# Single-pass up products, a shorter join and smaller rings in a fused graph-attention and feed-forward kernel

## The reference

```python
x = x + gnn(layernorm(x), src, dst, W, attn_l, attn_r, W_res)     # x: 50000 x 768, 25000 edges sorted by dst
x = x + ffn(layernorm(x)[None], ...)[0]
# gnn: ft = x_head @ W.T for 12 heads of 64; e = leaky_relu(a1[src] + a2[dst]);
#      alpha = softmax of e over the edges with one dst; agg = segment_sum(alpha * ft[src], dst)
#      return relu(agg + x_head @ W_res.T)
# ffn: gelu(x @ W1 + b1) @ W2 + b2 for all rows but the first six, which go through small experts
```

## Time and profile before

| what | value |
|---|---|
| median of 3 runs | 2991.76 us (2991.27 to 2992.91) |
| the profiled execution | 2989.99 us, span 2988.1 us |
| TensorE, share of the span | 96%, granted clock 0.978 |
| VectorE, ScalarE, GpSimd | 83%, 62%, 71% |
| VectorE uses the first scale (L1009) | at 46.56 us |
| edge loop, 600 to 1100 us | TensorE busy 499.88, VectorE 455.79, DMA share 0.78 |
| drain and join, 1130 to 1240 us | TensorE busy half of the time, clock 1.00 falling to 0.50 |
| node loop, 1500 to 2000 us | TensorE busy 498.94, VectorE 422.88, DMA share 0.87 |
| node loop, 1300 to 1350 us | TensorE busy 50.00 of 50, DMA share 0.94 |

### The profile page before, as it was taken

How to read it: one execution, slowest core, us unless ns; L and a number is a source line. 1 busy time by engine, 2 the same in 40 slices (tenths; PEclk the granted TensorE clock), 3 DMA queues, 4 the chain that set the end, 5 groups by cost and what they waited for, 6 DMA issues and landing times. The chain is left out here.

```text
span 2988.1 us, 65135 instructions
## 1 busy us (share of the span) xinstructions
PE 2866.0 (96%) x20124; PEld 2556.8 (86%) x20124; DVE 2486.9 (83%) x5828; ACT 1843.7 (62%) x3384; POOL 2125.9 (71%) x2027
## 2 busy tenths in 40 slices
PE   3999999999999996699999999999999999999998
PEld 3888888888888884588888888999989999899986
DVE  5699999999999976688888888888888888888883
ACT  2566666656666561467666767666676666667662
POOL 6766666666666610688888888888888888888882
PEclk9999999999999997699999999999999999999998
DMA  8899999898888725599888888888888888888873
GB/s 203 153 220 224 211 218 219 210 219 218 217 220 212 219 92 194 185 324 320 315 308 311 301 310 295 309 296 302 297 294 304 294 299 294 290 293 291 301 247 117
DMA packets 246616, 757.82 MB, mean 254 GB/s; under 512 B 78899, under 2 KB 81203, under 8 KB 246291
## 3 DMA queue, kind: packets, MB, share of 16 engines
q1 hardware_dynamic: 173900, 544.41, 51.5%
q0 software_dynamic: 69312, 209.33, 30.7%
q10 hardware_dynamic: 3176, 1.29, 0.2%
HBM read 623.04 MB, written 232.17 MB: 286 GB/s over the span
## 5 line engine op out<-in xcount | busy, mean ns | idle before, releaser
L670 ACT ACTIVATE arena<-ps 128x768 f32<-128x768 f32 x392 | 317.8, 811 | 532.5 <-PE ps L730 532.3
L891 PE MATMUL ps<-wr_bd,arena 128*128 128x128 f32 x4704 | 601.7, 278 | 27.5 <-DVE arena L1214 26.4
L891 PEld LDWEIGHTS ps<-wr_bd,arena 128*128 128x128 f32 x4704 | 566.8, 194 | 36.6 <-issue 34.6
L870 PE MATMUL ps<-arena,w_sb 128*96 128x256 f32 x2352 | 571.6, 379 | 0.0
L582 POOL DMA_INDIRECT arena<-agg_scratch,nrow x392 | 441.0, 1125 | 79.8 <-issue 73.2
L1209 DVE SCALAR_TENSOR_TENSOR ps<-ps,r_n,arena 128x768 f32<-128x768 f32 x392 | 400.8, 1022 | 62.5 <-DMA arena<-agg_scratch,nrow 39.3
L870 PEld LDWEIGHTS ps<-arena,w_sb 128*96 128x96 f32 x2352 | 362.3, 163 | 82.8
L560 POOL TENSOR_SCALAR arena<-csr_neg,mv,r_n 128x768 f32<-128x768 f32 x392 | 387.2, 988 | 50.9 <-POOL r_n L590 41.4
L621 ACT ACTIVATE arena<-ps 128x512 f32<-128x512 f32 x588 | 312.8, 593 | 119.9 <-PE ps L747 70.2
L1214 DVE SCALAR_TENSOR_TENSOR arena<-ps,arena 128x768 f32<-128x768 f32 x392 | 375.4, 958 | 13.4
L572 POOL TENSOR_SCALAR arena<-arena,nm_n,r_n 128x768 f32<-128x768 f32 x392 | 383.1, 977 | 1.0 <-issue 0.4
(11 more groups left out here) (198 smaller groups left out, 5526.6 us busy)
## 6 DMA issues: line engine op xcount, KB each, us to landing
arena<-in_x SPq DMA_DIRECT2D x196, 768.0 KB
arena<-in_x_cols SPq DMA_DIRECT2D x392, 384.0 KB
out<-arena SPq DMA_DIRECT2D x195, 768.0 KB, 5.2
agg_scratch<-arena SPq DMA_DIRECT2D x196, 384.0 KB
arena<-in_x,e_slot POOLq DMA_INDIRECT x392
arena<-agg_scratch,nrow POOLq DMA_INDIRECT x392
nrow<-row_scratch SPq DMA_DIRECT2D x196, 1.0 KB
row_scratch<-e_slot POOLq DMA_INDIRECT x189
```

The costliest lines, as they stand in the source:

```text
L870: last = nc.tensor.matmul(ps[0:HID, 6 + v, 0:PAIR * P], w1_sb[:, i, :], t2[:, v, i, :], start=(i == 0), stop=(i == NC - 1))
L891: last = nc.tensor.matmul(pair(1)[:, i * P:(i + 1) * P], xt_ring[:, g, i * P:(i + 1) * P], wr_bd[:], start=True, stop=True)
```

## The change

1. **Up as single-pass products.** w1 and the transposed tile are split into a high and a low part in `fp32r`: `w1_hi`, `w1_lo`, `t2_hi`, `t2_lo`. ScalarE writes `t2_hi` from PSUM, VectorE the rest into `t2_lo`, and up is hi*hi + lo*hi + hi*lo. `pair(0)` comes free only after `t2_lo`.
2. **Statistics.** bn_stats and its aggregate leave the node loop's VectorE; ScalarE does the copy with sum and the square for all tiles.
3. **Two masks.** dst transpose and mask move from step 9 to step 20, and `mask_ring` has 2 slots.
4. **Aggregated rows.** `agg_ring` has 2 rows; the last 10 chunks use 5 rows in the free end of `xs_ring`. SP waits for these before it loads x over them.
5. **Join in row layout.** Coefficients are transposed to chunks x heads, the last and first rows are scaled as they lie (98 x 1536), only the keep coefficient is spread over the features, one scan per feature block runs straight from PSUM, and the rows are transposed back and combined in two halves.
6. **First power.** For group 0 both powers are issued at GpSimd's step 8 and not 11 and 12.

The distances of gather, residual product and power in the node loop stay as they are. Core of the diff:

```diff
-        mask_ring = part(32424, BODY, P)
-        agg_ring = part(37544, G, D)
+        mask_ring = part(32424, 2, P)
+        agg_ring = part(35752, AR, D)          # AR = 2
+        agg_last = part(6912, LR, D)           # LR = 5, NL = 10
...
+                    if isinstance(b, int) and c == G + 1:
+                        pool.wait_ge(s_ve, 1)
+                        pool.tensor_tensor(r_a[:, 0, 0:2 * G:2], ve_a[:, 0, 0:2 * G:2], half[:, 0:G], ALU.pow)
+                        pool.tensor_tensor(r_a[:, 0, 1:2 * G:2], ve_a[:, 0, 1:2 * G:2], half[:, 0:G], ALU.pow)
...
# ScalarE, node loop
-                        nc.scalar.activation(t2[:, v, :, k * P:(k + 1) * P], pair(0)..., ACT.Copy)
+                        nc.scalar.activation(t2_hi[:, v, :, k * P:(k + 1) * P], pair(0)..., ACT.Copy)
-                    if u % PAIR == 1 and exists(t, NT):
+                    if exists(t, NT):                        # L701, and likewise L663
...
# TensorE, node loop
-                        at_least(pe, s_te2, tt)
+                        at_least(pe, s_lo2, tt)
                         transposes(pair(0), n2[:, (u - L_T2) % 2, :], s_tp2)
-                            last = nc.tensor.matmul(ps[0:HID, 6 + v, 0:PAIR * P], w1_sb[:, i, :], t2[:, v, i, :], ...)
+                            for n, (w, h) in enumerate(((w1_hi, t2_hi[:, v]), (w1_lo, t2_hi[:, v]), (w1_hi, t2_lo[:, v]))):
+                                last = nc.tensor.matmul(ps[0:HID, 6 + v, 0:PAIR * P], w[:, i, :], h[:, i, :], ...)
...
# VectorE, node loop, between y and the small tiles
+                        dve.wait_ge(s_te2, tl + 1)
+                        V.tensor_tensor(t2_lo[:, v, :, f], pair(0)..., t2_hi[:, v, :, f].bitcast(f32),
+                                        ALU.subtract).then_inc(s_lo2, 1)
-                        V.tensor_scalar(ve_n[:, w, 0:1], mv1[:, w, 1:2], EPS, None, ALU.add)
-                            V.bn_stats(bn1[:, u // PAIR % 2, h, :], x_ring[...])
-                        V.bn_aggr(mv1[:, w, 0:2], ...)
...
# VectorE, edge loop
-                        at_least(dve, d_agg[j], 16 * (2 * b + (i - L_AGG) // G))
+                        if not isinstance(b, int) or ca < EC - NL:
+                            at_least(dve, d_agg[v % AR], 16 * (BODY // AR * b + (i - L_AGG) // AR))
+                        elif ca >= EC - NL + LR:
+                            dve.wait_ge(d_agl[(ca - EC + NL) % LR], 16)
...
# join, VectorE
-            for j in range(NC):        # product, scan, product, product, add on 128 x 196
+            dve.wait_ge(d_last, 16)
+            V.tensor_tensor(o_last, o_last, coef_t[:, :, 0, :]..., ALU.mult)          # 98 x 1536
+            for j in range(NC):
+                V.tensor_tensor_scan(chain_o[:, j, 1:EC + 1], keep_b[:, j, :], ps[:, j // 2, ...], 0.0, ALU.mult, ALU.add)
+            for n in range(2):
+                V.tensor_tensor(fix_rows[:, n, :], back, coef_t[:, n, 1, :]..., ALU.mult)
+                V.tensor_tensor(fix_rows[:, n, :], fix_rows[:, n, :], o_first[:, n, :], ALU.add).then_inc(s_frow, 1)
```

More of the change, by code:

```diff
@@ L162, in gnn_ffn_kernel @@
         g_f = part(18856, EC, rows=HEADS)
[L163 to L167, removed]
+        coef_t = part(19052, 2, 3, HEADS, rows=EH)
+        chain_o = part(27000, NC, EC + 1)
+        keep_b = part(28200, NC, EC)
         o_last = part(22292, 2, D, rows=EH)
@@ L170, in gnn_ffn_kernel @@
         fix_rows = part(25364, 2, D, rows=EH)
[L171 to L175, removed]
+        pens = part(32680, 2, EC, rows=HEADS)
+        m_run = part(33072, EC + 1, rows=HEADS)
+        t_run = part(33270, EC + 1, rows=HEADS)
+        gap = part(33468, 4, EC, rows=HEADS)
+        coef = part(34252, 4, EC, rows=HEADS)
         w2_sb = part(21504, D, rows=HID + 1)
+        w1_sb = part(24000, NC, HID)
+        v_sb = part(24600, NC * (2 * HEADS + 2))
         w_dup = part(22272, P, rows=DH)
@@ L333, in gnn_ffn_kernel @@
         s_eo = sem("s_eo")
-        d_agg = [sem(f"d_agg{u}") for u in range(G)]
+        d_agl = [sem(f"d_agl{u}") for u in range(LR)]
+        d_agg = [sem(f"d_agg{u}") for u in range(AR)]
         d_tab = sem("d_tab")
@@ L450, in _ @@
                         q = b * (U // PAIR) + u // PAIR
+                        if isinstance(t, int) and t == (XR - LR) // PAIR * PAIR:
+                            for w in range(LR):
+                                sp.wait_ge(d_agl[w], 16 * (NL // LR))
                         at_least(sp, s_y, t - XR + PAIR)
@@ L531, in _ @@
                     gq = 2 * b + (i - 12) // G
-                    if k == 12 % G and exists(gq, NG):
+                    if k == 12 % G and exists(gq, NG) and not (isinstance(gq, int) and gq == 0):
                         w = (i - 12) // G % 2
@@ L535, in _ @@
                             .then_inc(s_rpd, 1)
[L537 to L538 removed]
+            for u in range(AR):
+                pool.wait_ge(d_agg[u], 16 * ((EC - NL) // AR))
+            for u in range(LR):
+                pool.wait_ge(d_agl[u], 16 * (NL // LR))
             pool.wait_ge(s_idx, 1)
@@ L815, in _ @@
             pe.wait_ge(s_coef, 1)
+            for a in range(3):
+                for n in range(2):
+                    last = nc.tensor.transpose(ps[0:EH, 7, (3 * n + a) * HEADS:(3 * n + a + 1) * HEADS],
+                                               coef[:, a + 1, n * EH:(n + 1) * EH], ident[0:HEADS, 0:HEADS])
+            last.then_inc(s_ctp, 1)
             pe.wait_ge(l_fix, 48)
@@ new lines, in _ @@
+            for j in range(NC):
+                dve.wait_ge(s_ftr, 2 * (j // 2) + 2)
+                dve.wait_ge(s_keb, 1)
+                V.tensor_tensor_scan(chain_o[:, j, 1:EC + 1], keep_b[:, j, :],
+                                     ps[:, j // 2, j % 2 * EC:(j % 2 + 1) * EC], 0.0,
+                                     ALU.mult, ALU.add).then_inc(s_fixt, 1)
+            for n in range(2):
+                back = (pair(3) if n == 0 else pair(0))[0:EH, :]
+                dve.wait_ge(s_ftb, n + 1)
+                link_up(V.tensor_tensor(fix_rows[:, n, :].rearrange("p (h d) -> p h d", h=HEADS),
+                                        back.rearrange("p (h d) -> p h d", h=HEADS),
+                                        coef_t[:, n, 1, :][:, :, None].to_broadcast([EH, HEADS, DH]), ALU.mult))
+                dve.wait_ge(s_ofirst, 1)
+                V.tensor_tensor(fix_rows[:, n, :], fix_rows[:, n, :], o_first[:, n, :], ALU.add).then_inc(s_frow, 1)
```

261 lines of the change are left out of this document (128 added, 133 removed).

## The result

| | before | after | ratio, 95% interval |
|---|---|---|---|
| median of 16 runs each | 2992.15 us (2983.14 to 2995.84) | 2979.36 us (2966.74 to 2988.51) | 0.9956 [0.9943, 0.9970] |
| the profiled execution | 2989.99, span 2988.1 | 2973.13, span 2971.3 | |

The change gains 13 us, or 0.4%, and the interval leaves out 1; forecast were 59. In the profiled executions 16.8 us went, and the timeline says where. The last chunk sum moves from 1164.25 to 1170.78 (+6.5, forecast +0.4). From there to the second store of corrected rows the join takes 29.65 us in place of 41.85 (-12.2, forecast -13). Another -0.4 lies between that store and the first z1. From the first z1 to the end it is 1762.2 in place of 1772.9 (-10.7, forecast -46). The miss is in the node loop.

A forecast was written before the change was run, and what follows sets the result against it. It took TensorE, busy without a gap, to bound both loops, with gathers barely in time. Node loop -46, drain +3.4, start -3 and join -13 summed to about -59 us: 2932 us, range 2875 to 3015.

The forecast's parts named there:

- the join: Between edge and node loops: fewer coefficient products and the new row-layout chain save 13 us, between 8 and 18.
- Up: Node loop, TensorE: nine single-pass products take 1.08 us in place of 1.31, making its tile 4.13 us.
- the subtraction: Node loop, VectorE: 768 columns from PSUM added for each tile, 0.87 us, at most 1.26.
- z1 to the next output store: Node loop, from an even tile's z1: VectorE's 3.83 + 4.05 and the queue 0.4 behind, 8.3 us.
- the landing in the gather loop's sum: Node loop: gathered row lands 8.2 to 8.8 us after the output store, giving 4.13 to 4.28 per tile; 4.24 taken.
- rival 1: Node loop: landing comes sooner, queues alone bound the tile at 4.10 to 4.15 us; -87 us, total 2890; chance 0.27.
- theory: Node loop: landing hangs on the burst of output store and load, hardly on the gather's issue; 4.2 to 4.3 us; chance 0.38.
- rival 2: Node loop: landing stays 8.20 us behind the gather's issue, tile 4.54 us, +68 us, total 3047; chance 0.18.
- The late gather of the earlier trace: Node loop near 2178 us: a gather issued 2.54 us after the store needed at most 6.15 us, so the burst decides.
- The drain: End of the edge loop, where VectorE sets the pace: some ten masks come on top, +3.4 us.
- The early power: Start: first power no longer queues behind the gathers of chunks 9 to 11; between 0 and -7.5 us, -3 taken.
- Rival 3: Edge loop: two sum rows stall it where a store needs 10.6 us; about +75 us, total 3005; chance 0.08.

The follow-up runs named there:

- e10: Changed kernel with the node loop's load of x rows cut to 16 of 128 partitions: 2899.22 us.
- e11: Changed kernel with both the output store and the load of x cut to 16 of 128 partitions: 2888.36 us.
- e1: Changed kernel with VectorE's three small operations for the power put ahead of the t2_lo subtraction, so the gather issues sooner: 2935.84 us, 0.986.
- e7: Kernel before, with two steps more between gather and residual product and the load of transposed columns moved two steps as well: 2974.21 us, 0.9955.
- e5: Changed kernel with two steps more between gather and residual product and the load of transposed columns moved two steps as well: 2887.17 us, 0.9657.
- e4: Changed kernel with the output store cut to 16 of 128 partitions: 2898.98 us.
- e3: Kernel before, with two steps more between gather and residual product, transposed-column load not moved: 2999.11 us, 1.0083.

## Why the prediction was right in its parts and wrong in its sum

**Right.** Up costs 1.13 us where 1.08 was forecast, the subtraction 0.87; z1 to the next output store 8.35, forecast 8.3. The wait is on even tiles and for the gathered row. The join gave -12.2, forecast -13; but that is one trace, and the new join took 25.2 to 30.9 us in the nine traces with the whole load of x, 23.35 and 23.12 in e10 and e11, against 41.8 in the three of the old one.

**The step that failed** is the landing in the gather loop's sum, "Four tiles then need 8.3 + 8.2 to 8.8, or 4.13 to 4.28 per tile", from which 4.24 was taken. The form of the sum is right: four tiles are 8.35 + 8.99 = 17.34 us, or 4.34, and 4.35 was measured between 1500 and 2500. The landing was mis-sized. 8.2 matches no distance from the store in the rows; it is the one from the gather's issue. 8.8 stood as the upper end, but is the median of the waiting tiles before, whose longest is 9.23. It grew to 8.99 with the gather issued 1.6 us behind the store in place of 0.5. 4.35 in place of 4.24 over 380 tiles is 42 us, or 34 by the 4.33 of the stretch to 2900; 35 of the 46 expected are missing.

Why the upper end is the one that counts can be seen in e1, where every landing is recorded: store to landing is 8.1 us at the median of all 117 even gathers, just under the range, and 8.6 where z1 waited (45 of them). With 8.1 the sum would give 4.13 us per tile, and e1 took 4.26. The likely reason is that a late landing stops TensorE and an early one gives nothing back, since a tile can't be shorter than TensorE's own. In a steady loop, the waiting tiles must carry the sum, not the range below them.

**What the forecast never did** is to put the same sum to the kernel before: 8.60 + 8.81 = 17.41 us for four tiles, 4.35. TensorE's own tile there is 4.33, as e7 shows, and not the 4.36 that the forecast took for it: the gather loop was already as long as TensorE's tile, and by some 0.02 us the longer one. (In the tiles that did not wait for the row, z1 to the store was mostly 9.10, as it is throughout in e7, where no z1 waits for a row.) The 26.5 us of wait did not mean that the loop was nearly free. Shortening TensorE alone could give almost nothing. With the loop opened, the same change takes the tile from 4.33 to 4.11, and 82 us off the node loop (e5 against e7), where rival 1 had 87.

**Between theory and rival 2.** Rival 2 has z1 to gather at 9.95 us, measured 9.97. Its landing of 8.20 after issue was 7.38 where z1 waited, just under the 7.5 that it names as the line between gain and loss. Its sum, 9.97 + 7.38 = 17.35 us, is the same loop as the forecast's 17.34, counted from the gather in place of the store: the sign came out right by 0.1 us. The e1 gather, issued 0.9 us earlier, landed 0.3 earlier, so both the burst and the own issue count, the burst for the larger part. e4, e10 and e11 show the bytes of store and load as the cause, the load's for the larger part: at most 3.3 us of the landing are the gather's own, and 7.4 is what the whole burst makes of it in e1. The late gather of the earlier trace rows was read rightly, as a hint that the burst matters, but one such row gives an upper bound for one tile and no median.

The Trainium skill's rule in "DMA: Bandwidth & Descriptors" (section on queues, rings and completion order) is that an engine goes round robin between its queues, packet by packet. The prediction took from it that the gather would not stand behind the whole burst. The measurement decides: in the 4 us after the issue GpSimd's queue moves 15 KB in e1 and 124 KB in e11, and the landing goes from 3.3 to 7.4 us. Whether the rule fails here, or one turn of SP's queue is that long, no run tells.

**The smaller terms.** The drain, 184th to last sum, is 38.5 us before and 39.4 to 42.1 with the change (median 40.1 of eleven traces): +0.9 to +3.6, forecast +3.4. But e3 and e7, which have the old edge loop, took 39.6 and 38.3, so the low end is within the spread of the old one. That the masks cause it was not tried by itself. The early power gave nothing (forecast -3): 128.72 against 129.10 with it. Rival 3 was right in its mechanism and far off in size: the landings of a sum row are late in a few places of the first sixty chunks only, for 1 to 13 us and not for 75, because a landing of 10.6 us is there the exception (8.0 at the median in e1, then 5.2) and not the rule.

## What to carry to other kernels

Before a bound is relieved, work out the period of each loop through DMAs (issue, landing, consumer, next issue) in the kernel as it is; a small wait can mean that this loop is exactly as long as the engine's tile, and then the relief gives nothing. Put the landings of the tiles that waited into that sum, and take them from the landing events where the trace has them: the start of a consumer that didn't wait is only an upper bound. Move a consumer further behind its gather together with everything in the same issuing queue: a load that waits for a slot held longer delays the store issued behind it, and the wait only changes its name. A ring that is cut because a transfer's median landing fits can still stall in the stage where the queues are fullest.

## What the runs showed of the hardware

- A gathered 128 x 768 row tile, issued 0.7 us behind the first of two transfers of 0.75 MB on SP's queue, lands 7.4 us after its issue (e1); 1.5 us behind, with the store cut to an eighth, 6.0 (e4), with the load cut 4.8 (e10), with both cut 3.3 (e11). In the first 4 us it moves 15 KB in e1 and 124 KB in e11.
- A median landing hides the tail: the 384 KB store of a sum row took 8.0 us at the median and up to 12.4 before 460 us, 5.2 behind that (e1).
- VectorE and GpSimd do not overlap on two 98 x 1536 products of two operands each: 1.76 and 2.77 us alone, 4.15 or 4.20 for whoever comes second.
- The same start lasts 10 us longer in some of these traces than in others (first chunk sum at 116.4 to 117.7 or at 126.9 to 130.1 us), with the kernel before as with the changed one. The short ones are the four traces of e1 to e4. What makes it was not looked for.
